# Eight experts over all tokens, or 23 tiles of gathered tokens, in a two-layer decoder on one core

## The reference

```
shared = silu(xf @ shared_w1.T) * (xf @ shared_w2.T) @ shared_w3.T      # hidden 1024
scores = sigmoid(xf @ router_w.T)                                       # [2048, 8]
_, top_idx = top_k(scores + expert_bias, 2)
mask = one_hot(top_idx, 8).sum(axis=-2)
gates = scores * mask
h1, h2 = split(einsum('td,ehd->teh', xf, w12), 2)                       # 8 experts, hidden 256
h = silu(h1) * h2 * gates[:, :, None]
routed = einsum('teh,edh->td', h, w3)
x = layernorm(x + shared + routed)
```

## Time and profile before

| what | value |
|---|---|
| median of three runs | 1788.09 us |
| profiled execution | 1784.82 us |
| its span in the profile | 1782.8 us |
| mean granted clock of TensorE (1.0 is 2.4 GHz) | 0.93 |
| busy: PE matmul, weight load, DVE, ACT, POOL | 88%, 72%, 55%, 36%, 24% |
| feed-forward stage, first up matmul to the first transposes of layer 1 | 479.25 to 913.3 us |

### The profile page before, as it was taken

One profiled execution on the slowest core, in us unless ns is written; L12 is line 12 of the kernel. 1 busy time (PEld: TensorE's weight loads), 2 busy tenths in 40 slices (PEclk: granted clock), 3 DMA queues, 4 the chain that ended last, 5 costly groups with the idle time before them and its releaser, 6 DMA issues.

```text
span 1782.8 us, 29530 instructions
## 1 busy us (share of the span) xinstructions
PE 1563.3 (88%) x12930; PEld 1284.5 (72%) x12930; DVE 972.0 (55%) x1762; ACT 643.9 (36%) x727; POOL 433.8 (24%) x402
## 2 busy tenths in 40 slices
PE   6899999999698999999987997997997995888786
PEld 5788887878587888888874884884784783555554
DVE  5666756667355333333355566566457453565574
ACT  3445434544321333333223433433442441314223
POOL 2320300202222544543320250251232223000000
PEclk9999999999888999999989998998998995778788
DMA  5000000000500100100000000000000011101000
GB/s 220 1 1 1 1 1 1 1 1 1 212 1 19 36 18 19 36 19 1 1 1 1 1 36 1 1 37 1 1 20 17 1 36 71 37 1 60 2 13 13
DMA packets 8768, 42.09 MB, mean 24 GB/s; under 512 B 1088, under 2 KB 3392, under 8 KB 7744
## 3 DMA queue, kind: packets, MB, share of 16 engines
q1 hardware_dynamic: 8640, 40.21, 6.0%
HBM read 31.82 MB, written 8.39 MB: 23 GB/s over the span
## 4 chain that ended last, share of the span: by engine, by line
PE 72%; DVE 20%; ACT 4%; issue 2%; POOL 1%; DMA 1%; SPq 0%; POOLq 0%; DVEq 0%; ACTq 0%
PE ps L111 15%; PE ps L112 14%; PE ps L113 14%; DVE sm L1301 8%; PE ps L546 6%; PE ps L838 4%; PE ps L844 3%; DVE m L1290 3%; PE ps L551 3%; PE ps L678 3%; PE ps L558 3%; PE ps L662 2%; PE ps L819 2%; ACT m L1013 2%; PE ps L953 1%
## 5 line engine op out<-in xcount | busy, mean ns | idle before, releaser
L1013 ACT ACTIVATE m<-ps 77x1024 f32<-77x1024 f32 (+4 forms) x248 | 184.0, 759 | 359.5 <-PE ps L113 160.9
L1301 DVE TENSOR_REDUCE sm<-ps 128x8 f32<-128x2048 f32 (+1 forms) x128 | 193.6, 1536 | 59.0 <-PE ps L819 40.6
L1290 DVE TENSOR_TENSOR m<-m,ps 128x1024 f32<-128x1024 f32 (+1 forms) x80 | 90.7, 1138 | 213.9 <-PE ps L113 189.1
L1780 POOL TENSOR_SCALAR sm<-sm 128x2 f32<-128x2 f32 x40 | 8.8, 219 | 761.9 <-DVE sm L1319 761.9
L1847 POOL TENSOR_TENSOR r<-m,r 128x1024 fp32r<-128x1024 f32 x48 | 115.3, 2402 | 262.9 <-ACT r L1013 262.9
L1187 ACT ACTIVATE m<-ps 128x2048 f32<-128x2048 f32 x64 | 119.3, 1877 | 143.6 <-PE ps L838 143.6
L546 PE MATMUL ps<-cst,m 128*77 128x128 f32 (+2 forms) x1008 | 142.1, 284 | 25.9 <-DVE m L1290 6.4
L111 PE MATMUL ps<-xTall,uw 128*128 128x512 f32 x384 | 152.0, 396 | 6.4 <-DVE xres L1290 4.9
L546 PEld LDWEIGHTS ps<-cst,m 128*77 128x77 f32 (+2 forms) x1008 | 116.2, 149 | 57.2 <-issue 17.5
L112 PE MATMUL ps<-xTall,uw 128*128 128x512 f32 x384 | 151.5, 395 | 0.0
L113 PE MATMUL ps<-xTall,uw 128*128 128x512 f32 x384 | 150.7, 392 | 0.0
(11 more groups left out here) (182 smaller groups left out, 3734.1 us busy)
## 6 DMA issues: line engine op xcount, KB each, us to landing
raw<-wu_dram SPq DMA_DIRECT2D x12, 768.0 KB, 4.3
keep_dram<-m SPq DMA_DIRECT2D x8, 768.0 KB, 3.3
m<-keep_dram SPq DMA_DIRECT2D x8, 768.0 KB, 4.3
w1raw<-w_dram SPq DMA_DIRECT2D x1, 3840.0 KB, 14.4
w0raw<-w_dram SPq DMA_DIRECT2D x2, 1024.0 KB, 19.6
w1f<-w1f_dram SPq DMA_DIRECT2D x1, 2048.0 KB, 18.8
out_dram<-xres SPq DMA_DIRECT2D x16, 128.0 KB, 1.8
w0raw<-w_dram SPq DMA_DIRECT2D x3, 512.0 KB, 6.3
```

Of the source, the lines that this page charges most:

```text
L1013: return act.activation(o, i, ACT.Copy)
L1290: return dve.tensor_tensor(o, a, b_, op)
L1301: return dve.tensor_reduce(o, i, AX.X, op, **kw)
```

## The change

The shared block keeps its four units (NS = 4; NU stays 12 only as the number of weight blocks). The eight expert units over all tokens go, and in their place stand 23 tiles (NT) of 256 rows. 23 is enough for any choice of two experts by 2048 tokens: 4096 rows are 16 full tiles, and each of eight experts can leave one tile partly filled, of which seven more tiles hold the worst case.

- **Scores and choice.** The scores of all tokens are multiplied ahead of the shared units. DVE copies x into the room of `w1f` (`xc`), ranks the scores in four passes, and PE counts with 32 fp32 matmuls how many tokens before this one chose the same expert (`slots_of`). DVE turns the counts into a row number for each token's first and second expert (`row`), a gate for each (`gateAB`), and the expert of each tile (`expert`).
- **Scatter.** POOL issues 32 indirect DMAs; each writes 128 rows of 1 KB of x to their places in the DRAM tensor `xs`. At the program's start SP fills `xs` with zeros.
- **Shared units.** The low part of the product moves from POOL to DVE. The scores' small matmuls are no longer between the turns.
- **Tile loop.** For each tile SP reads the expert's number into a register, fetches 768 KB of weights at an address made from it, fetches 256 KB of tokens and stores 256 KB of results in `ys`. The fetches of weights run four tiles ahead, with three raw and four split buffers. PE turns the tokens and does 24 up and 12 down matmuls of 256 columns; ACT, DVE and POOL split and multiply.
- **Gather.** POOL issues 32 indirect DMAs, each reading 128 rows of `ys`: eight at the end of the loop (batches 0 and 1), the others in layer 1's self attention, four per batch. DVE adds them to x with the gates (`routed_add`) ahead of the layer norm.
- `w1f` is fetched after the scatter.

```diff
+NS = 4
+NU = NE + NS
+NT = 23
...
+            sp.wait_ge(*zeroed.at("zero"))
+            for a in (0, 23):
+                sp.dma_start(xz[:, a:a + 23, :], zero.unsqueeze(1).to_broadcast([P, 23, 256])).then_inc(d_zero, 16)
...
+            def fetch_of(j):
+                e = sp.value_load(expert[0:1, j:j + 1], min_val=0, max_val=NE - 1)
...
+                else:
+                    sp.wait_ge(*r_pool.at("w", j - 3))
+                    sp.wait_ge(*r_dve.at("w", j - 3))
+                sp.dma_start(rraw[j % 3], wu_in[:, bass.ds(e * UW, UW)]).then_inc(d_u[j % 3], 16)
+            def tokens_of(j):
+                if j > 2:
+                    sp.wait_ge(*r_pe.at("xT", j - 3))
+                sp.dma_start(rx[j % 3], xsv[j]).then_inc(d_xs[j % 3], 16)
+            def store_of(j):
+                sp.wait_ge(*r_dve.at("y", j))
+                sp.dma_start(ysv[j], ry[j % 2]).then_inc(d_ys[j % 2], 16)
...
+            for j in TILES:
+                if j:
+                    store_of(j - 1)
+                if j + 3 < NT:
+                    tokens_of(j + 3)
+                if j + 4 < NT:
+                    fetch_of(j + 4)
+            store_of(NT - 1)
...
+            for j in TILES:                       # PE
+                up_of(j)
+                if j + 2 < NT:
+                    turn_tokens(j + 2)
+                if j:
+                    down_of(j - 1)
+            down_of(NT - 1)
...
+            for j in TILES:                       # ACT
+                act.activation(rhf[s], bank(streams[s], 1), ACT.Silu).then_inc(r_act.up("silu", j), 1)
+                act.wait_ge(*r_dve.at("h", j))
...
+                copy(rh[s][0], rhf[s]).then_inc(r_act.up("hi", j), 1)
+                if j + 2 < NT:
+                    turned_tokens(j + 2)
+                if j + 3 < NT:
+                    split_of(j + 3)
...
+            for j in TILES:                       # DVE
+                tt(rhf[s], rhf[s], bank(streams[s], 2), ALU.mult).then_inc(r_dve.up("h", j), 1)
+                dve.wait_ge(*r_act.at("hi", j))
+                tt(rh[s][1], rhf[s], rh[s][0].bitcast(F32), ALU.subtract).then_inc(r_dve.up("lo", j), 1)
+                if j + 2 < NT:
+                    turned_tokens(j + 2)
+                if j:
+                    outputs_of(j - 1)
+                if j + 3 < NT:
+                    split_of(j + 3)
...
+            def split_of(j):                      # POOL, the first 1024 of 1536 columns; DVE has the last 512
+                pool.wait_ge(*r_act.at("w", j))
+                pool.tensor_tensor(ruw[j % 4][1][:, 0:1024], rraw[j % 3][:, 0:1024], ruw[j % 4][0][:, 0:1024].bitcast(F32), ALU.subtract).then_inc(r_pool.up("w", j), 1)
...
+            scatter(range(0, 4))
+            split_unit(2)
+            scatter(range(4, 8))
+            weights1(0, 1)
+            scatter(range(8, 12))
+            weights1(2)
+            split_unit(3)
+            scatter(range(12, 16))
+            weights1(3, 4, 5, 6)
+            split_of(0)
...
+            for i in range(2):
+                pool.wait_ge(d_ys[i], 16 * ((NT + 1 - i) // 2))
+            for st in streams:
+                gather(st, st.batches[0])
```

More of the change, by code:

```diff
@@ L174, in program @@
         vm, vmi, mhalf, lift = (part(cst, PC, n) for n in ("vm", "vmi", "half", "lift"))
+        upper, k256, iota = (part(cst, PC, n) for n in ("upper", "k256", "iota"))
         streams = []
@@ L298, in ffn_act @@
             return o
-        MOE = [(n, k) for n in range(NU) for k in range(2)]
+        MOE = [(n, k) for n in range(NS) for k in range(2)]
         def moe_pe():
@@ new lines, in up_of @@
+            def up_of(j):
+                st = streams[j % 2]
+                up = tuple(k2(w[:, 0:1024]) for w in ruw[j % 4])
+                pe.wait_ge(*r_dve.at("xT", j))
+                pe.wait_ge(*r_dve.at("w", j))
+                pe.wait_ge(*r_pool.at("w", j))
+                for i, h in enumerate(("h1", "h2")):
+                    if j < 2 and i == 0:
+                        pe.wait_ge(*st.moe_act.at(NS - 1, 1, "silu"))
+                    elif j < 2:
+                        pe.wait_ge(*st.moe_dve.at(NS - 1, 1, "acc"))
+                    elif i == 0:
+                        pe.wait_ge(*r_dve.at("h", j - 2))
+                    for c in range(2):
+                        for q in range(2):
+                            m = mm3(pe, bank(st, 1 + i)[:, 256 * c:256 * (c + 1)], cols(up, A, q, slice(256 * i + 128 * c, 256 * i + 128 * (c + 1))), cols(rxT[j % 2], A, q), q == 0, q == 1)
+                    m.then_inc(r_pe.up(h, j), 1)
@@ L792, in _ @@
+            for st in streams:
+                turn_tokens(st.i)
+                down(st, NS - 1, 1, 1)
+            for j in TILES:
[5 more added lines that the diff above has]
+            down_of(NT - 1)
             last_moe(pe)
@@ L1461, in norm_only, with te @@
             def norm_only(st, b):
+                routed_add(st, b)
                 yield from layernorm(st, b, st.n_dve, st.n_pool, room=n_room(st))
                 yield
+            for t in range(8):
+                r = dve.tensor_copy(xc[:, 512 * t:512 * (t + 1)], xres[:, 512 * t:512 * (t + 1)])
+            r.then_inc(gate_dve.up("x"), 1)
+            rb = part(wr, PR, "rb")
+            def te(v):
+                return v.rearrange("p (t e) -> p t e", e=8)
+            for st in streams:
+                dve.wait_ge(*gate_act.at("th", st.i))
@@ L1529, in _ @@
-            together([*[moe(st) for st in streams], *[gating(st) for st in streams]])
+                    if turn == 7 and st.i == 1:
+                        turned_tokens(0)
+                    dve.wait_ge(*st.moe_act.at(n, k, "hi"))
+                    tt(st.r[2][:, 1024:2048], hf, st.r[2][:, 0:1024].bitcast(F32), ALU.subtract).then_inc(st.moe_dve.up(n, k, "lo"), 1)
+                    if turn == 6 and st.i == 1:
+                        split_of(0)
+                    if turn == 0 and st.i == 1:
+                        slots()
@@ new lines, in moe, with outputs_of @@
+                    yield
+            together([moe(st) for st in streams])
+            down(streams[0], len(MOE) - 1)
+            turned_tokens(1)
+            split_of(1)
+            down(streams[1], len(MOE) - 1)
+            split_of(2)
+            def outputs_of(j):
+                dve.wait_ge(*r_pe.at("dn", j))
+                if j > 1:
+                    dve.wait_ge(d_ys[j % 2], 16 * (j // 2))
+                dve.tensor_copy(ry[j % 2], bank(streams[j % 2], 3)).then_inc(r_dve.up("y", j), 1)
@@ L1532, in _ @@
+            outputs_of(NT - 1)
+            together([norm_only(st, st.batches[0]) for st in streams])
             last_moe(dve)
@@ L1863, in _, with scatter, split_of @@
-            together([*[moe(st) for st in streams], weights1()])
+            def scatter(tiles):
+                for t in tiles:
+                    for e in range(2):
+                        pool.indirect_dma_start(xs, bass.IndirectOffsetOnAxis(ap=row[:, 16 * e + t:16 * e + t + 1], axis=0), xc[:, 256 * t:256 * (t + 1)], None).then_inc(d_sc, 16)
+            def split_of(j):
+                pool.wait_ge(*r_act.at("w", j))
+                pool.tensor_tensor(ruw[j % 4][1][:, 0:1024], rraw[j % 3][:, 0:1024], ruw[j % 4][0][:, 0:1024].bitcast(F32), ALU.subtract).then_inc(r_pool.up("w", j), 1)
@@ new lines, in _, with gather @@
+            for j in range(1, NT):
+                split_of(j)
+            def gather(st, b):
+                for e in range(2):
+                    for j in range(2):
+                        k = 16 * e + 2 * b + j
+                        pool.indirect_dma_start(g_rows(st)[e][j], None, ys, bass.IndirectOffsetOnAxis(ap=row[:, k:k + 1], axis=0)).then_inc(d_g[st.i], 16)
+            for i in range(2):
+                pool.wait_ge(d_ys[i], 16 * ((NT + 1 - i) // 2))
+            for st in streams:
+                gather(st, st.batches[0])
```

375 lines of the change are left out of this document (255 added, 120 removed).

## The result

The changed kernel takes 1713.08 us (median of 4 runs, 1710.04 to 1716.22) against 1785.73 (4 runs, 1780.72 to 1789.34): a ratio of 0.9595, with a 95% interval of 0.956 to 0.963, about 73 us less. The prediction was 1710. The profiled execution has a span of 1713.6 us against 1782.8, so there are 69.2 us to account for.

A forecast was written before the change was run, and what follows sets the result against it. PE was taken to bound the kernel, busy 88% of the span. −100.0 − 2.5 + 3 + 14 + 8 = −77.5 from 1784.8 gave 1707.3, so 1710 for the median; forecast 1680 to 1738 (0.62), range 1652 to 1768.

The forecast's parts named there:

- The bound on PE: Tile loop: PE's own work, 36 matmuls and four transposes, takes 4.8 us a tile, 110 us for 23 tiles.
- The tokens' round: Tile loop: result copied, stored, later tokens fetched, turned, multiplied down, next result copied; 6.5 us a tile, bounds 5.6 to 8.1.
- The weights' round: Tile loop: store, register load, weight fetch, ACT's copy and DVE's work close over two tiles; 12.3 us, 6.1 a tile.
- The 7.2 us that I took for a tile: Tile loop: DVE blocked by POOL's weight split, 7.2 us a tile, 165.6 for 23 tiles, 100.0 less than before.
- the filling of the loop: Start of the tile loop: a raw buffer frees only after stream 0's last down projection; +3 us.
- Ahead of the loop: Scores, ranking, count and shared units before the tile loop: 157 us against 159.6, a change of −2.5 us.
- the low part costs DVE 1.2 us a turn: hidden: Shared units: the low part, now on DVE, takes 1.2 us of a turn of 8.3 and adds no time.
- Scatters: POOL, during the shared units: 32 indirect DMAs at 1.5 us each, hidden up to 3.3 us each.
- rival C: Indirect DMAs on POOL make the kernel slower than before, e.g. 1794 us at 4.0 each; chance 0.06, shared with another rival.
- Behind the loop: Last matmul to layer 1: result, store, eight gathers, adds and norm take 23 us, +14 against before.
- Layer 1: Layer 1: 24 gathers on POOL and 24 adds on DVE cost 8 us of 47; bounds 0 and 47.
- Rival B: Tile loop: gaps bring PE to half clock, about 9 us a tile, 41 us more, 1751 us; chance 0.16.

The follow-up runs named there:

- e1: Changed kernel with the store of results issued behind both fetches (tokens and weights) in SP's loop; 1687.90 us, ratio 0.9470 to the kernel before.
- g1: Changed kernel with only the tokens' fetch moved ahead of the store in SP's loop, weights still behind it; 1707.59 us, ratio 0.9556 to the kernel before.
- e4: Changed kernel with the tile's weights fetched from a constant address, without the register load on SP; 1708.71 us, ratio 0.9575 to the kernel before.
- f2: Changed kernel with POOL's part of the loop's weight split cut from 1024 to 64 columns from tile 4 on; 1710.62 us, ratio 0.9596.
- e3: Changed kernel with one of the three products of each score matmul, 32 matmuls in place of 96; 1699.33 us, ratio 0.9506 to the kernel before.
- f3: Changed kernel with the count's totals folded into the prefix-sum matmuls, 18 in place of 32; 1708.67 us, ratio 0.9589 to the kernel before.
- e2: Changed kernel with POOL's splits of w1 issued singly, between scatters or behind DVE's low parts; 1693.94 us, ratio 0.9510 to the kernel before.
- f5: Changed kernel with layer 1's adds of routed rows, batches 2 and up, over 8 columns in place of 256; 1708.04 us, ratio 0.9578.

## Why the prediction came out right, step by step

The total came out by luck: two steps failed by 23 and 26 us in opposite directions, and the range was wide enough for what was left.

- **The bound on PE** (4.8 us a tile): right. With the store out of the way tiles come every 5.00 us (e1).
- **The tokens' round**, worked out at 6.5: measured 6.04 in its shortest form, from the same terms. The landing was 2.8 (2.7 and 0.4 in the forecast), and from the transposes to the copied tile 2.83, where I had 0.5 + 1.6 + 0.7 + 0.1 = 2.9. The issue of the store was 0.37.
- **The weights' round**, 12.3 for two tiles: 12.50 in the trace, and about 12.4 by g1's 11.70 and the 0.75 more ahead of the fetch. The register load was 1.0 where I took 0.5 (e4), and the fetch with what is ahead of it 4.3 where I took 4.8.
- **The 7.2 us that I took for a tile: the step that failed.** I let DVE lose the race for the weight split, with 2.4 us of hold in the round. In the trace DVE starts it 0.05 ahead of POOL and takes 0.69. What is held is the low part, by 0.7, and that costs the tile 0.15 to 0.34 (f2). The two rounds without the hold, 6.1 to 6.5, were the better number: 6.43. In 23 tiles this is 18 of the 23 us; the filling of the loop, +3, wasn't seen either: 145.3 / 6.43 is 22.6 tiles. On the rule of the Trainium skill ("SBUF — State Buffer", Who interferes with whom): the low part agrees with it (two SBUF inputs, held), and so does the product (one input from PSUM: 0.68 at 727.38, inside POOL's 2.88 from 726.82), which POOL doesn't hold.
- **Ahead of the loop, −2.5 forecast, +23.8 measured: the other step that failed.** The score matmuls, 18.9 in place of 10.8: the earlier trace rows has their price at full clock (1.00 from 490 to 492 us), and here they ran at 0.55 (8 us; e3 shows that they aren't hidden). The count, 9.6 in place of 5, as fp32 counts twice and its totals ran near half clock (f3). Together that is 13 of the 26. The rest is the hold of DVE by POOL: "the low part costs DVE 1.2 us a turn: hidden" is true only alone. The working weighed the hold for the loop and not for the shared units, where POOL has the same splits of w1 as before and DVE a new operation of two SBUF inputs. By e2 it is worth 13.4 us, 9.5 of waits and 3.9 of clock. That makes 26 in all, though f3 shows that the pieces aren't quite independent.
- **Scatters**: 32, most of them 0.96 us, some up to 2.0, in the mean 1.09, and 0.30 to the next; I took 1.5. Hidden, as forecast; rival C falls.
- **Zeros**: nothing; hidden in layer 0.
- **Behind the loop, 23 forecast, 20.7 measured:** gathers at 1.25 in place of 1.5 are 2 us of it. The Trainium skill ("DMA: Bandwidth & Descriptors", Latency and other measured facts) gives about 1 us to the first byte. The row's 0.95 is near it, though it is POOL's time on the operation and not the time to a byte, and the 0.30 between two comes on top.
- **Layer 1, +8 forecast, +10.4 measured:** right in size as far as it is known: in the ten kernels whose layer 1 isn't edited it is 5.3 to 14.5 over the 574.4 of before. f5 points to the adds, not to the gathers, without proving it.
- **Clock in the loop**: 0.98, as forecast; PE was 80% busy. Rival B falls.

## What to carry to other kernels

When a loop is paced by rounds through an in-order DMA queue, work out every round with the queue's order: a store that waits for the newest result must not stand ahead of fetches that don't need it. Where two rounds are about equally long, shortening one gives little, and both together give much more than the sum (6.43 falls to 5.94 or 6.20 with one, to 5.00 with both). An edit that shows in its loop's trace can be lost in the time, when the rest of the kernel varies by several us. An operation that reads two SBUF operands on DVE must be checked against every POOL burst beside which it now lands, not only in the stage that is being designed.
